# First projection of a graph layer: ScalarE rounds q's three parts a turn later, VectorE adds skip and k ahead of its weight units, magnitudes early and signs late

## The reference

```python
xn = _layernorm(x, axis=-1)
q = (x @ Wq[l] + bq[l]).reshape(N, H, D)
k = (x @ Wk[l] + bk[l]).reshape(N, H, D)
v = (x @ Wv[l] + bv[l]).reshape(N, H, D)
...
x = agg + (x @ Ws[l] + bs[l]) + enc
...
wg = w.reshape(o, i // group_size, group_size)
scale = jnp.mean(jnp.abs(wg), axis=-1, keepdims=True) + EPS
wq = jnp.clip(jnp.round(wg / scale), -1.0, 1.0) * scale
```

## Time and profile before

| what | us |
|---|---|
| median of 3 runs | 3349.69 (3349.22 to 3351.88) |
| the profiled execution, its own time | 3346.05 |
| span of its trace | 3344.3 |
| first product of turn 1 to the start of the edge phase | 100.64 to 388.46 |

### The profile page before, as it was taken

One profiled execution on the slowest core, in us unless ns is written; L12 is line 12 of the kernel. 1 busy time (PEld: TensorE's weight loads), 2 busy tenths in 40 slices (PEclk: granted clock), 3 DMA queues, 4 the chain that ended last, 5 costly groups with the idle time before them and its releaser, 6 DMA issues. The chain is left out here.

```text
span 3344.3 us, 46214 instructions
## 1 busy us (share of the span) xinstructions
PE 2558.1 (76%) x10373; PEld 1750.8 (52%) x10373; DVE 2347.1 (70%) x4332; ACT 1239.1 (37%) x6570; POOL 1708.9 (51%) x1618
## 2 busy tenths in 40 slices
PE   2888866664988869996666668878077799869998
PEld 1766522222765547872222256655056576657776
DVE  5777687778977767767777798777834346476665
ACT  0344378776000011007777700000233232155554
POOL 0101377777777751117777777777400235344444
PEclk8999998988899999998888879999588899989999
DMA  1544577776777775437777767777130323261111
GB/s 41 182 151 163 175 237 236 239 237 195 204 219 226 228 224 161 133 122 240 236 235 239 229 188 224 223 226 221 55 101 13 126 101 114 73 201 38 38 38 37
DMA packets 228144, 549.19 MB, mean 164 GB/s; under 512 B 32920, under 2 KB 50946, under 8 KB 227918
## 3 DMA queue, kind: packets, MB, share of 16 engines
q0 software_dynamic: 106240, 348.21, 35.4%
q1 hardware_dynamic: 110158, 177.31, 15.8%
q10 hardware_dynamic: 11520, 20.98, 1.8%
HBM read 471.88 MB, written 74.49 MB: 163 GB/s over the span
## 5 line engine op out<-in xcount | busy, mean ns | idle before, releaser
L1189 POOL DMA_INDIRECT edge_ring<-v_rows,edges_src x664 | 655.3, 987 | 202.3 <-issue 160.9
L1352 PE MATMUL edge_psQ<-layer_q_space,layer_y_space 128*128 x1992 | 553.2, 426 | 268.1 <-DVE layer_y_space L1220 266.7
L1189 POOL DMA_INDIRECT edge_ring<-k_rows,edges_src x664 | 628.3, 946 | 252.1 <-issue 141.9
L1389 PE MATMUL edge_psA<-layer_q_space,edge_hot 128*128 128x256 f32 (+1 forms) x2656 | 652.6, 398 | 130.9 <-DVE edge_hot L1284 82.8
L1308 ACT ACTIVATE layer_y_space<-layer_y_space 128x64 f32<-128x64 f32 x2656 | 637.2, 241 | 234.3 <-DVE layer_y_space L1220 233.2
L1389 PEld LDWEIGHTS edge_psA<-layer_q_space,edge_hot 128*128 128x128 f32 x2656 | 491.2, 193 | 292.0 <-issue 224.8
L1295 DVE TENSOR_TENSOR layer_q_space<-edge_ring,edge_psQ 128x512 f32<-128x512 f32 x664 | 456.7, 688 | 149.9 <-DMA edge_ring<-v_rows,edges_src 144.4
L1220 DVE TENSOR_TENSOR layer_y_space<-edge_psQ,edge_ring 128x512 f32<-128x512 f32 x664 | 433.8, 685 | 177.9 <-DMA edge_ring<-k_rows,edges_src 165.0
L1352 PEld LDWEIGHTS edge_psQ<-layer_q_space,layer_y_space 128*128 128x128 bf16 x1992 | 211.0, 106 | 610.4 <-issue 512.5
L103 PE MATMUL proj_psP<-proj_w,proj_xT 128*128 128x512 f32 x1920 | 480.4, 409 | 43.9 <-DVE proj_enc L867 32.3
L1308 ACT ACTIVATION_READ_ACCUMULATOR layer_y_space<-layer_y_space 128x1 f32 x2656 | 494.9, 186 | 0.0
(11 more groups left out here) (287 smaller groups left out, 3047.3 us busy)
## 6 DMA issues: line engine op xcount, KB each, us to landing
layer_y_space<-local_rows SPq DMA_DIRECT2D x82, 256.0 KB, 4.5
edge_ring<-k_rows,edges_src POOLq DMA_INDIRECT x664, 3.9
edge_ring<-v_rows,edges_src POOLq DMA_INDIRECT x664, 3.7
base_rows<-proj_enc SPq DMA_DIRECT2D x40, 256.0 KB, 2.0
k_rows<-proj_out ACTq DMA_DIRECT2D x40, 256.0 KB, 3.1
v_rows<-proj_out ACTq DMA_DIRECT2D x40, 256.0 KB, 4.2
ffn_downT<-down_rows SPq DMA_DIRECT2D x11, 512.0 KB, 9.6
agg_rows<-layer_y_space SPq DMA_DIRECT2D x20, 260.0 KB, 3.9
```

Of the source, the lines that this page charges most:

```text
L1189: pool.indirect_dma_start(ring[:, n % NB, :], None, k_dram if n < USED else v_dram, bass.IndirectOffsetOnAxis(ap=T["src"][:, s:s + 1], axis=0)
L1352: last = pe.matmul(psQ[i][:], hotT[j % 2][:, i * P:(i + 1) * P], one(qp[:, k, bass.ds(tiles[i], 1), :]), start=(k == 0), stop=(k == 2))
L1389: last = pe.matmul(psA[:, bass.ds(d % 2, 1), e, 0:hi - lo].rearrange("p o w -> p (o w)"), hot[:, s % R, :], wv[:, s % R, lo:hi], start=Fal ...
```

## The change

Only `normalise_project` changes. In words:

- q's split: ScalarE forms the three bf16 copies (`q_part`), VectorE keeps the two subtractions (`q_less`). Both work on the tile of the turn before, between the pieces at the beginning of the turn. A new semaphore `rounded` joins them, `split` counts the subtractions.
- VectorE adds skip and k before `size_up`, v after it, and q behind `choose` and `low_unit`.
- `size_and_sign` is cut in two: `size` stands where it was, `sign` behind the copies of the turned units and behind the store of k.
- The next sum into q's output buffer waits for the last part of the tile two turns before.

```diff
+                def q_part(i, k):
+                    if k:
+                        act.wait_ge(split, i * 2 + k)
+                    else:
+                        act.wait_ge(ready, i * 4 + Q_ + 1)
+                    act.copy(qp[:, k, i, :], out[:, i % 2, Q_ - 1, :]).then_inc(rounded, 1)
+
                 for i in range(NT):
                     if i + 1 < NT:
                         high(i + 1)
+                    if i:
+                        q_part(i - 1, 0)
                     if i + 2 < NT:
                         ln.root(act, i + 2)
+                    if i:
+                        q_part(i - 1, 1)
                     for u in units(i):
-                        size_and_sign(u)
+                        size(u)
+                    if i:
+                        q_part(i - 1, 2)
                     for u in units(i - 1):
                         take(u)
-                    for j, dram in ((K_, k_dram), (V_, v_dram)):
-                        act.wait_ge(ready, i * 4 + j + 1)
-                        act.dma_start(dram[i * P:(i + 1) * P, :], out[:, i % 2, j - 1, :]).then_inc(kv_out[i % 2], 16)
+                    act.wait_ge(ready, i * 4 + K_ + 1)
+                    act.dma_start(k_dram[i * P:(i + 1) * P, :], out[:, i % 2, K_ - 1, :]).then_inc(kv_out[i % 2], 16)
+                    for u in units(i):
+                        sign(u)
+                    act.wait_ge(ready, i * 4 + V_ + 1)
+                    act.dma_start(v_dram[i * P:(i + 1) * P, :], out[:, i % 2, V_ - 1, :]).then_inc(kv_out[i % 2], 16)
+                for k in range(3):
+                    q_part(NT - 1, k)
...
+                def q_less(i, k):
+                    q = out[:, i % 2, Q_ - 1, :]
+                    vec.wait_ge(rounded, i * 3 + k + 1)
+                    vec.tensor_tensor(q, q, qp[:, k, i, :], ALU.subtract).then_inc(split, 1)
+
+                def add(i, j):
+                    b = i % 2
+                    vec.wait_ge(projected, i * 4 + j + 1)
+                    if j == S_:
+                        vec.wait_ge(biased, i + 1)
+                        vec.tensor_tensor(enc[:, b, :], psP[j][:], enc[:, b, :], ALU.add).then_inc(ready, 1)
+                        return
+                    if i >= 2 and j == K_:
+
+                        vec.wait_ge(kv_out[b], i // 2 * 32)
+                    if i >= 2 and j == Q_:
+                        vec.wait_ge(rounded, (i - 1) * 3)
+                    vec.tensor_tensor(out[:, b, j - 1, :], psP[j][:], bias[:, j, :], ALU.add).then_inc(ready, 1)
+
                 for i in range(NT):
-                    b = i % 2
                     if i + 1 < NT:
                         low(i + 1)
+                    if i:
+                        q_less(i - 1, 0)
                     if i + 2 < NT:
                         normalise(i + 2)
+                    if i:
+                        q_less(i - 1, 1)
+                    add(i, S_)
+                    add(i, K_)
                     for u in units(i):
                         size_up(u)
+                    add(i, V_)
                     for u in units(i):
                         choose(u)
...
+                    for u in units(i - 1):
+                        low_unit(u)
+                    add(i, Q_)
+                for k in range(2):
+                    q_less(NT - 1, k)
```

More of the change, by code:

```diff
@@ L596, in normalise_project @@
         base_out = [m.sem(f"base_out{b}") for b in range(2)]
-        turned, xT_ready, projected, ready, split, biased = (
-            m.sem(s) for s in ("turned", "xT_ready", "projected", "ready", "split", "biased"))
+        turned, xT_ready, projected, ready, split, rounded, biased = (
+            m.sem(s) for s in ("turned", "xT_ready", "projected", "ready", "split", "rounded", "biased"))
         qp = T["q_parts"]
@@ L745, in high, with size @@
                     act.copy(xT[:, i % 2, 0].rearrange("p k n -> p (k n)"), psT[i % 2][:]).then_inc(xT_high, 1)
-                def size_and_sign(u):
+                def size(u):
                     act.wait_ge(unit_in[u % RAW], u // RAW * 16 + 16)
@@ L756, in size_and_sign, with sign @@
                                        accum_out=sums[:, u, c:c + 1]).then_inc(sized, 1)
+                def sign(u):
                     act.wait_ge(sized, (u + 1) * KC)
```

## The result

| | before | changed |
|---|---|---|
| median of the runs, us | 3350.78 (4 runs, 3349.22 to 3354.1) | 3300.06 (4 runs, 3299.97 to 3302.38) |
| the profiled execution, us | 3346.05 | 3300.06 |
| first product of turn 1 | 100.64 | 101.73 |
| last 72 products (v of turn 18 and on) | 366.10 | 319.61 |
| between the two: the stage | 265.46 | 217.88 |

A forecast was written before the change was run, and what follows sets the result against it. No engine was full; a chain through VectorE and ScalarE held PE in the first projection. With PE setting 12.5 us turns, a 47.8 us gain less 0.6 lost at the end took 3349.7 to 3302.5 us, range 3297 to 3315.

The forecast's parts named there:

- The floor of a turn, 12.5 us: First projection: PE's turn without waits, 12.14 us plus a 0.38 us step; the kernel before took 15.36.
- the chain above it: First projection: one chain through VectorE and ScalarE, with PE at its end, kept turns 2.9 us over PE's shortest.
- The positions on VectorE: Times in VectorE's turn, from PE's first product: skip's sum done at about 6 us, v's sum at 9.5.
- d: Time at which VectorE starts its turn, counted from the start of PE's skip product: 1.05 us.
- The end: After the last turn of the first projection, q's split across two engines has nothing to hide it: loss 0.6 us.
- The loop of 12.0 us and the slack of 6: First projection: longest loop not passing PE averages 12.0 us; skip's sum comes 6 us before PE needs it.
- Units in time: SP's loads of weight units, issued at 13.5 to 15 us, land in 3 us, just in time for the magnitudes at 16.9.
- rival A: Late unit loads make the loop through SP set turns of 13.1 us: 3307 us in all; chance 0.20.
- POOL: Its 1.29 us sum now falls in VectorE's wait for V: cost taken as 0, at most 1.1 us per turn.
- the 3.64 us: Whole kernel: the median of the runs lies this far above the profiled execution; added to the forecast.

The follow-up runs named there:

- the spare operations: Changed kernel with three or five extra, repeated VectorE subtractions per turn in `low`: medians 3934.63 and 3955.31 us, against 3967.33 for the kernel before.
- e10: The changed kernel run again, unaltered, against the kernel before on the same chip: 3300.02 against 3350.52 us, ratio 0.9847.
- e5: Changed kernel with each unit's sign back right behind its magnitudes, against the kernel before on its chip: 3916.54 against 3967.33 us, ratio 0.9877.

## Why the prediction was right

The forecast was 3302.5 us, in a range of 3297 to 3315, and 3300.06 were measured. The stage is where the mechanism shows, and there 47.8 us were predicted and 47.6 measured.

- *The floor of a turn, 12.5 us, and the chain above it.* Right: 12.51 in all 16 turns, granted clock 1.00. To turn 18 it is 259.44 - 211.84 = 47.6 us, to the last 72 products 265.46 - 217.88 = 47.6. The edge phase starts at 342.51, where 341 was predicted; most of the rest is turn 0, which ends between 100.1 and 102.7 us in the runs here, whatever the edit.
- *The positions on VectorE.* Right: v at 9.56 (9.5), d = 0.95 (1.05), skip done at 5.7 (6.05). ScalarE's copy to bf16 is 0.604 us in the median, inside 0.52 to 0.63.
- *The end.* The three copies and two subtractions across two engines last from 337.42 to 340.79, 3.4 us, where the split on VectorE had three copies of 0.43 and two subtractions, 2.8 with the steps between. The predicted loss of 0.6 fits.
- *The loop of 12.0 us and the slack of 6.* Right in kind: the spare operations give a loop of 11.6, so 12.0 was a little high, and a slack of 6.3 to 6.5, so 6 was a little low.
- *Units in time.* The landing was mis-sized: 3 us were taken, and the units take 3.3 to 4.3 in the median. It cost nothing: ScalarE waited 1.9 us in all, in 5 waits, and PE not once. By the prediction's own sum a landing under 3.6 us is free, and one of 4.5 loses only 0.6 per turn against the slack; so rival A was close, and never reached PE. The Trainium skill, "DMA: Bandwidth & Descriptors", section "Anatomy of one DMA — SWDGE (gpsimd) path", gave the estimate of 2.6 us for a unit alone. The traces do not reach it: the nearest medians are those of the kernel with its rounding moved and its loads first, 2.7 to 3.0.
- *POOL.* Its sum starts 7.9 us into the turn (183.84), in VectorE's wait, as predicted. One choice was held, 1.38 us instead of 0.35, at the very start, before turn 1: the choices begin at 112.04 and POOL's sum at 112.2.
- *Which part does it.* The prediction gave one sum for all parts. The experiments split it: order 43.3 of 47.6 us, by an earlier buffer and earlier loads together; rounding adds the last 4 when the order is new, and 0.8 when it is old; the signs nothing, or a loss of 12.5 in the old order. Parts of one chain do not add: the rounding with the loads ahead gives 42.6 by itself as well.

What stays open is the difference of 3 us between the stage and the medians, on the first chip as in the runs e10 and e5. The forecast had carried the 3.64 us between the profiled execution of before and its median over to the changed kernel, whose profiled execution is itself at the median; without them it would have been 3298.9. The predicted gain was 47.2 us and the medians give 50.7, so that the forecast of the whole time came within 2.4 us is in part luck; that of the stage is not. Executions do differ by this much outside the stage: the two traces of the changed kernel have the same stage, and from the start of the edge phase on 2955.9 and 2959.2 us. Why the medians lie 3 us further apart than the stages was not pursued.

## What to carry to other kernels

Write down the shortest possible turn of the fullest engine, and the longest loop through the others; once the loop is under the turn (here 11.6 under 12.5), more relief is worth nothing (the place of the signs: 0.0 us). Above it, what decided here was when the sum came that frees the full engine's buffer, and what stood behind that sum in the queues. Count the queue that issues the loads as a member of the loop: in two of the kernels here 13 and 42 us lay in loads that stood behind a wait for a result that they did not need. Idle time of an engine is no measure of slack; adding an operation a few times, and reading the turn, is.

## What the runs showed of the hardware

The first projection takes the same time where the whole kernel before takes 3351 us and where it takes 3967: the stage of a kernel at PE's bound is 217.88 and 217.89 us in the two traces of the changed kernel on the quick side, and 217.90 with the signs together on one of the slower chips. On the other slower chip no kernel was at PE's bound throughout, but the first turns of the order-only kernel take the same 12.5 us. The difference lies in the two edge phases with their gathers. The changed kernel and the one with the signs together compare like this: first edge phase, to the run of products at the start of the second projection, 886.9 and 1192.6 us; second projection, to the second edge phase, 225.5 and 225.5; second edge phase, to the last product into `edge_psA`, 848.8 and 1156.5; all the rest behind it 994.8 and 995.6. In the window from 345 to 1200 us, inside the first edge phase of both, the changed kernel moves 224 GB/s and the other 164:

```profile
345.00:1200.00 855.00, 609.09 (x2354) 362.12 (x2372) 672.04 (x1317) 361.13 (x2729) 639.50 (x662) 0.92 0.75 224
```

```profile
345.00:1200.00 855.00, 470.04 (x1544) 238.59 (x1564) 477.65 (x845) 371.47 (x2678) 461.98 (x489) 0.74 0.56 164
```

A GpSimd gather instruction takes as long there (0.946 us in the median in both), so it is not GpSimd's issuing that is slower; what is, no run here shows. So a gain in one stage is better read in us of that stage than as a ratio of the whole: the runs e10 and e5 have nearly the same gain in the median, 50.5 and 50.8 us, and the ratios 0.9847 and 0.9877.
